# Order of the first tiles in a ternary feed-forward kernel: q between x's first tiles, x's third half transposed and summed, c's first halves rounded on GpSimd

## The reference

```python
q_emb = relu(cond @ W3 + b3)                      # 128 x 256
v_sum = sum(x, axis=1)                            # over the 32 places of a sequence
c = relu(((32 * x + v_sum) * q_emb[:, None]) @ W2 + b2)

def ternary_quant(w):                             # value used: -s, 0 or s
    s = mean(abs(w)); return clip(round(w / s), -1, 1) * s
h1 = c @ ternary_quant(w1).T
h3 = c @ ternary_quant(w3).T
out = x + (silu(h1) * h3) @ ternary_quant(w2).T
```

## Time and profile before

| | us |
|---|---|
| median of 3 runs | 166.16 |
| profiled execution, its own time | 166.31 |
| span of its profile | 164.5 |
| TensorE busy | 160.6 (98%) |
| VectorE busy | 116.1 (71%) |
| ScalarE busy | 88.9 (54%) |
| GpSimd busy | 55.2 (34%) |

### The profile page before, as it was taken

The page is one execution under the profiler, slowest core; times in us unless marked ns, Lnnn a source line. Parts: engine busy times, 40 slices in busy tenths (PEclk is TensorE's granted clock), DMA queues, the critical chain, the costliest instruction groups (busy, mean ns, idle before and its releaser), DMA issues.

```text
span 164.5 us, 2291 instructions
## 1 busy us (share of the span) xinstructions
PE 160.6 (98%) x765; PEld 132.5 (81%) x765; DVE 116.1 (71%) x186; ACT 88.9 (54%) x163; POOL 55.2 (34%) x52
## 2 busy tenths in 40 slices
PE   7999999999999999999999999999999999999992
PEld 3988777888887888788887888788887888788892
DVE  2166999988978891888548891888647880666863
ACT  3148788525744566355744566255744567255540
POOL 5014033321361266204841266203841267001600
PEclk9999999999999999999999999999999999999999
DMA  5998656666566597000160006000160006100063
GB/s 155 298 357 158 103 81 96 97 98 100 90 98 96 91 234 130 11 4 0 23 104 0 0 4 112 17 0 0 22 108 4 2 0 108 19 0 4 15 112 128
DMA packets 67412, 12.67 MB, mean 77 GB/s; under 512 B 63216, under 2 KB 67144, under 8 KB 67400
## 3 DMA queue, kind: packets, MB, share of 16 engines
q1 hardware_dynamic: 67104, 12.33, 38.1%
q10 hardware_dynamic: 296, 0.20, 0.5%
HBM read 8.32 MB, written 4.19 MB: 76 GB/s over the span
## 4 chain that ended last, share of the span: by engine, by line
PE 98%; DVE 0%; issue 0%
PE bank L516 49%; PE bank L559 21%; PE bank L444 17%; PE bank L543 3%; PE bank L429 3%; PE bank L478 1%; PE bank L459 1%; PE bank L491 1%; PE bank L471 0%; PE bank L453 0%; DVE xo L746 0%; PE bank L481 0%; PE bank L483 0%; PE bank L487 0%; DVE blank L688 0%
## 5 line engine op out<-in xcount | busy, mean ns | idle before, releaser
L516 PE MATMUL bank<-c_hi,T 128*128 128x512 f32 (+1 forms) x176 | 69.2, 393 | 0.0
L516 PE MATMUL bank<-c_lo,T 128*128 128x512 f32 (+1 forms) x176 | 68.8, 391 | 0.0
L380 ACT ACTIVATE silu<-bank,checked 128x512 f32<-128x512 f32 (+1 forms) x48 | 33.1, 689 | 51.5 <-PE bank L516 51.3
L731 DVE SCALAR_TENSOR_TENSOR gf<-bank,out_scale,silu 128x512 f32<-128x512 f32 (+1 forms) x42 | 31.3, 744 | 34.4 <-PE bank L516 30.8
L516 PEld LDWEIGHTS bank<-c_hi,T 128*128 128x128 f32 (+1 forms) x176 | 32.7, 186 | 7.6 <-issue 0.2
L516 PEld LDWEIGHTS bank<-c_lo,T 128*128 128x128 f32 (+1 forms) x176 | 32.8, 186 | 7.3
L268 POOL TENSOR_TENSOR x<-y,qT 128x512 f32<-128x512 f32 x12 | 13.7, 1144 | 53.3 <-DVE y L649 53.3
L444 PE MATMUL bank<-x,W_sb 128*128 128x256 f32 x128 | 29.3, 380 | 0.0
L559 PE MATMUL bank<-g_hi,T 128*128 128x512 f32 x70 | 28.5, 407 | 0.0
L739 DVE TENSOR_TENSOR g_lo<-gf,g_hi 128x512 fp32r<-128x512 f32 x40 | 28.4, 711 | 0.0
L387 ACT CAST g_hi<-gf 128x512 fp32r<-128x512 f32 x40 | 24.5, 612 | 5.4 <-DVE gf L731 5.1
(11 more groups left out here) (71 smaller groups left out, 113.9 us busy)
## 6 DMA issues: line engine op xcount, KB each, us to landing
xb<-in_x_dram SPq DMA_DIRECT2D x64, 64.0 KB, 2.5
out_dram<-turned SPq DMA_DIRECT2D x28, 128.0 KB, 2.7
xo<-in_x_dram SPq DMA_DIRECT2D x3, 256.0 KB, 4.3
w_sb<-in_L_ffn_w_dram SPq DMA_DIRECT2D x2, 384.0 KB, 5.9
w_sb<-in_L_ffn_w_dram SPq DMA_DIRECT2D x1, 682.0 KB, 7.7
w_sb<-in_L_ffn_w_dram SPq DMA_DIRECT2D x2, 256.0 KB
xo<-in_x_dram SPq DMA_DIRECT2D x1, 512.0 KB, 3.9
xo<-in_x_dram SPq DMA_DIRECT2D x2, 128.0 KB, 2.6
```

The costliest lines, as they stand in the source:

```text
L380: nc.scalar.activation(silu[r, m % 2, :], h1[j % 2][r], ACT.Silu, scale=checked[r, 0:1]).then_inc(silu_done, 1)
L516: last = pe.matmul(dst[j % 2][0:w, :], T13[:, k, col:col + w], part[:, g % NC, k, :], start=(i == 0), stop=(i == len(passes) - 1))
L731: nc.vector.scalar_tensor_tensor(out=gf[r, m % 3, :], in0=second, scalar=out_scale[r], in1=silu[r, m % 2, :], op0=ALU.mult, op1=ALU.mult). ...
```

## The change

- TensorE: the two matmuls of q and the transpose of the biases come between the two tiles of `mix_x(0)`, q first. Two blank matmuls follow `mix_x(0)`. `mix_x(2)` moves behind `project_c(0)`.
- The third half (`SUMMED = 2`) is no longer multiplied by `mix`: TensorE only transposes its four blocks (with the identity), and VectorE sums them over the sequence, adds 32 x, and multiplies by q from SBUF.
- `c_hi` of the first two halves is written by GpSimd, ahead of each `c_lo`, and no longer by VectorE.
- The first half of `w1`'s absolute sum goes from VectorE to ScalarE, behind `relu(0)`.
- SyncE issues the load of `W2` ahead of the load of x's third half, and does its two semaphore increments for `o_free` after these loads, not ahead of all.

```diff
@@ sync
-            for free in o_free:
-                sp.sem_inc(free, 1)
...
             load_half(1)
+            sp.dma_start(W2_sb[:], W2.rearrange("(c p) n -> p c n", p=P)).then_inc(got_W2, 16)
             load_half(2)
-            sp.dma_start(W2_sb[:], W2.rearrange("(c p) n -> p c n", p=P)).then_inc(got_W2, 16)
+            for free in o_free:
+                sp.sem_inc(free, 1)
@@ gpsimd
             for n in range(EARLY):
-                pool.wait_ge(early_hi_done, n + 1)
+                if n < HALVES:
+                    pool.wait_ge(relu_done, DC * (n + 1))
+                    nc.gpsimd.tensor_copy(half_of(c_hi, n), ct[:, n % NCT]).then_inc(first_hi_done, 1)
+                    pool.wait_ge(first_hi_done, n + 1)
+                else:
+                    pool.wait_ge(early_hi_done, n - HALVES + 1)
@@ scalar
             relu(0)
+            abs_sum(0, w1_sb, 0, got_w1[0], 16)
             abs_sum(0, w1_sb, 1, got_w1[1], 32)
@@ tensor, mix_x(n)
                 for t in range(HTT):
+                    if n == 0 and t == 1:
+                        project_q()
+                        transpose_b()
...
+                        if n == SUMMED:
+                            last = pe.transpose(there, rows, ident[:])
+                        else:
+                            last = pe.matmul(there, rows, mix[:], start=True, stop=True)
@@ tensor
             mix_x(0)
-            pe.wait_ge(got_b, 16 * 2)
-            pe.transpose(b_cols_ps, b_rows[:], ident[0:2 * DC, 0:2 * DC]).then_inc(b_cols_done, 1)
...
+            keep_busy(2)
             mix_x(1)
-            mix_x(2)
             pe.wait_ge(got_W2, 16)
             project_c(0)
+            mix_x(2)
             project_c(1)
@@ vector, scale_mixed(n)
+                if n == SUMMED:
+                    dve.wait_ge(y_done, 1)
+                whole = flat(y[:, n % 2]) if n == SUMMED else mixed_of(n)
+                nc.vector.tensor_tensor(by_batch(flat(x1[:, n % 2])), by_batch(whole),
                                         over_sequence(flat(qT[:, n])), ALU.mult).then_inc(x1_done, 1)
@@ vector
             scale_mixed(0)
             scale_mixed(1)
-            abs_sum(0, w1_sb, LOADED * D, got_w1[0])
-            scale_mixed(2)
-            early_hi(0)
+            sum_sequence(SUMMED)
+            add_sum(SUMMED)
+            scale_mixed(SUMMED)
             limit(0)
             above_limit(0, w1_sb, w1_t, parts[0])
             scale_mixed(3)
-            early_hi(1)
```

More of the change, by code:

```diff
@@ L41, in adaln_ternary_ffn_kernel @@
     EARLY = AHEAD * HALVES
+    SUMMED = 2
     NCT = 4
@@ L167, in adaln_ternary_ffn_kernel @@
         checked_done = sem("checked_done")
-        early_hi_done, early_lo_done = sem("early_hi_done"), sem("early_lo_done")
+        first_hi_done, early_hi_done, early_lo_done = sem("first_hi_done"), sem("early_hi_done"), sem("early_lo_done")
         wT_done = sem("wT_done")
@@ L264, in scale_by_q @@
             def scale_by_q(n):
-                pool.wait_ge(y_done, n - EARLY + 1)
+                pool.wait_ge(y_done, n - EARLY + 2)
                 pool.wait_ge(z_done, n - 1)
@@ L427, in mix_x, with project_q, transpose_b @@
                     for c in range(DC):
[L428 to L431, removed]
-                last.then_inc(mixed_done, 1)
+                        there = mixed[:, c * HT + t * P:c * HT + (t + 1) * P]
+                        rows = kept(n // HALVES)[:, n % HALVES * HTT + t, c * P:(c + 1) * P]
+                        if n == SUMMED:
+                            last = pe.transpose(there, rows, ident[:])
+                        else:
+                            last = pe.matmul(there, rows, mix[:], start=True, stop=True)
+                last.then_inc(mixed_done, 1)
+            def project_q():
+                pe.wait_ge(got_W3, 16)
+                pe.wait_ge(condT_copied, 1)
+                for c in range(DC):
+                    pe.matmul(qT_ps[:, c, :], W3_sb[:, c * P:(c + 1) * P], condT[:], start=True, stop=True
+                              ).then_inc(q_done, 1)
+            def transpose_b():
+                pe.wait_ge(got_b, 16 * 2)
+                pe.transpose(b_cols_ps, b_rows[:], ident[0:2 * DC, 0:2 * DC]).then_inc(b_cols_done, 1)
             def project_c(n):
@@ L448, in sum_partitions @@
             def sum_partitions(k):
-                if k != 1:
-                    pe.wait_ge(first_abs_done, 1 + k // 2)
-                pe.wait_ge(abs_done, (1, 3, 4)[k])
+                if k == 2:
+                    pe.wait_ge(first_abs_done, 1)
+                pe.wait_ge(abs_done, (2, 4, 5)[k])
                 pe.matmul(sums_ps[k], ones[:], abs_sums[:, k, :], start=True, stop=True).then_inc(sums_done, 1)
@@ L481, in _, with keep_busy @@
             pe.transpose(condT_ps, cond_sb[:], ident[:]).then_inc(condT_done, 1)
-            for _ in range(2):
-                pe.matmul(bank[:, 7, 0:P], blank[:], blank[:], start=True, stop=True)
+            def keep_busy(n):
+                for _ in range(n):
+                    pe.matmul(bank[:, 7, 0:P], blank[:], blank[:], start=True, stop=True)
+            keep_busy(2)
             pe.wait_ge(mix_ready, 6)
             mix_x(0)
-            pe.wait_ge(got_b, 16 * 2)
-            pe.transpose(b_cols_ps, b_rows[:], ident[0:2 * DC, 0:2 * DC]).then_inc(b_cols_done, 1)
[L488 to L492, removed]
+            keep_busy(2)
             mix_x(1)
-            mix_x(2)
             pe.wait_ge(got_W2, 16)
             project_c(0)
+            mix_x(2)
             project_c(1)
@@ L626, in scale_mixed @@
             def scale_mixed(n):
-                dve.wait_ge(mixed_done, n + 1)
+                if n != SUMMED:
+                    dve.wait_ge(mixed_done, n + 1)
                 if n >= 2:
                     dve.wait_ge(z_done, n - 1)
-                nc.vector.tensor_tensor(by_batch(flat(x1[:, n % 2])), by_batch(mixed_of(n)),
+                if n == SUMMED:
+                    dve.wait_ge(y_done, 1)
+                whole = flat(y[:, n % 2]) if n == SUMMED else mixed_of(n)
+                nc.vector.tensor_tensor(by_batch(flat(x1[:, n % 2])), by_batch(whole),
                                         over_sequence(flat(qT[:, n])), ALU.mult).then_inc(x1_done, 1)
@@ L635, in transpose_x, with transposed, nth_summed @@
                 if n >= EARLY + 2:
-                    dve.wait_ge(y_done, n - EARLY - 1)
+                    dve.wait_ge(y_done, nth_summed(n - 2))
                 nc.vector.transpose(flat(xT[:, n % 2]), flat(xb[:, n])).then_inc(xT_done, 1)
+            def transposed(n):
+                return mixed_of(n) if n == SUMMED else flat(xT[:, n % 2])
+            def nth_summed(n):
+                return 1 if n == SUMMED else n - EARLY + 2
             def sum_sequence(n):
-                dve.wait_ge(xT_done, n - EARLY + 1)
-                nc.vector.tensor_reduce(vsum[:, n % 2, :], by_batch(flat(xT[:, n % 2])), AX.X, ALU.add).then_inc(vsum_done, 1)
+                if n == SUMMED:
+                    dve.wait_ge(mixed_done, n + 1)
+                else:
+                    dve.wait_ge(xT_done, n - EARLY + 1)
+                nc.vector.tensor_reduce(vsum[:, n % 2, :], by_batch(transposed(n)), AX.X, ALU.add).then_inc(vsum_done, 1)
             def add_sum(n):
-                dve.wait_ge(vsum_done, n - EARLY + 1)
-                if n >= 2 + EARLY:
-                    dve.wait_ge(x1_done, n - 1)
+                dve.wait_ge(vsum_done, nth_summed(n))
+                if n >= EARLY:
+                    dve.wait_ge(x1_done, max(n - 1, SUMMED + 1))
                 nc.vector.scalar_tensor_tensor(
-                    out=by_batch(flat(y[:, n % 2])), in0=by_batch(flat(xT[:, n % 2])), scalar=float(S),
+                    out=by_batch(flat(y[:, n % 2])), in0=by_batch(transposed(n)), scalar=float(S),
                     in1=over_sequence(vsum[:, n % 2, :]), op0=ALU.mult, op1=ALU.add).then_inc(y_done, 1)
```

## The result

The changed kernel takes 166.75 us (median of 22 runs, 166.05 to 168.35), the kernel before 166.15 (22 runs, 165.56 to 168.29): a ratio of 1.0051, 95% interval 1.0032 to 1.0071. It is slower by 0.5%, just clear of zero and just beyond the 0.3% that I had called no change.

What follows compares the result with a forecast made beforehand. TensorE was taken to bound the kernel, full up to `h1`. Reordering and cheaper transposes gave -0.10 us, the third product's wait for GpSimd +0.42, sum +0.32: forecast 166.5 us, range 165.9 to 167.0.

Steps and rivals of the forecast that it cites:

- The mechanism that I gave the highest chance: Ahead of the third projection: one lost wait of VectorE's third-half product for GpSimd, 0.24 to 0.72 us; chance 0.57.
- The wait for GpSimd: VectorE's third-half product with q waits out GpSimd's first subtraction, ends 0.55 us behind it; TensorE loses 0.42 us.
- my formula: Price of the third product's wait as a function of GpSimd's cast time C: C - 0.28 us.
- The transposes at half of the cost: Third half, behind the first projection: four transpose records take 0.46 us instead of 0.93 with `mix`, plus 0.10 for switching.
- That GpSimd doesn't keep VectorE out twice: Against the rival that `above_limit` of `w1` also waits out GpSimd's next cast and subtraction: 167.3 us, chance 0.08.
- The semaphore increments of SyncE: SyncE's first loads: moving the increments behind them makes loads 0.1 us earlier, which nothing waits for; effect 0.
- The same 8 + 1 + 4 records: TensorE from 3.53 to 6.69: `mix_x(0)`, biases and q reordered at the same cost; 0, range 0 to +0.2 us.
- `W2` at no gain: Even issued as before, `W2` lands at 7.66, ahead of the first projection's start at 7.82.
- that TensorE is full up to `h1`: TensorE's timeline to `h1` at 17.33 has no hole above about 0.15 us, so VectorE's wait for q costs nothing.
- what would upset it: Sign of being wrong: records halve their time at a different moment, moving all that follows by half that difference.

Runs made afterwards that it cites:

- the version with both edits: Changed kernel with SyncE's increments ahead of its loads again and GpSimd's first subtraction held until VectorE's third-half product with q: 165.76 us, ratio 0.9967.

## Why the prediction was right, and where it wasn't

The time of 166.75 lies in the range, and the sign is that of the forecast; 166.5 is also the median of the changed kernel's usual executions. The mechanism that I gave the highest chance is shown: its row, its hole, and the 0.47 us that come back when GpSimd is held. But the sum came out by two misses of opposite sign, +0.3 and -0.3, and that they nearly cancel was luck.

- *The wait for GpSimd*: right. The cast took 0.61 (I took 0.70 between 0.52 and 1.27), the product 1.47, ending 0.57 behind the subtraction (0.55). VectorE was ready 0.35 us behind the start of the subtraction in the usual profile (I had 0.3). The hole is 0.34 (0.42, or by my formula at 0.61, 0.33). Removing the collision gave 0.47 in the times and 0.41 in the traces, from the first projection to `h1`; that this is my 0.42 again is in part chance, since I had the cast 0.09 too long.
- *The transposes at half of the cost*: right. Four records in 0.43 us at the fast level, and exchanging them for `mix` against the wait changed the time by no more than the scatter (0.1).
- *That GpSimd doesn't keep VectorE out twice*: right. They alternate.
- *"The semaphore increments of SyncE: 0.1 us earlier loads, for nothing that is waited for. All these at 0"*: wrong, by 0.3 us. The load of x's first tile, issued 0.13 us sooner, pushed cond's landing from 2.2 to 2.6 us. TensorE had next to nothing to spare there: before, cond landed at about 2.93 and its transpose followed the blanks at 3.09; after, it landed at about 3.33 and the transpose began at 3.49. That cost 0.3 us in the usual executions of this order (0.30 without the held subtraction, 0.25 with it). I had looked at who waits for the earlier loads, and not at which other loads land near them. What the two loads share, so that one holds up the other, no run here shows.
- *"The same 8 + 1 + 4 records ... in another order, at the same cost", and `W2` at no gain*: wrong. With the two faults taken out the change is 0.4 us faster than the kernel before, where I had 0.1. q between the tiles is worth 0.7 in that version, `W2` ahead about 0.45. These two don't add up: the kernel before has neither and is only 0.4 slower, not 1.15, so each is the price of going without it while the other is there. The step that failed is the first: that TensorE is full up to `h1`. It is full in the one execution that I had, in which its records halve their time at 6.7. By the lengths of the rows in the 13 other profiles this comes between 3.7 and 5.5 us in seven, between 6.7 and 7.1 in four, and near 10 in the two late ones. Where it comes early TensorE is through with its work sooner than the loads, q's relu and the first product, and waits for them: 0.56 us for the product in one, 0.33 for the biases in another. What shortens that chain then pays. I had also asked only `W3` whether it comes in time for q between the tiles (it was waited for in one profile of nine, 0.61 us), and not the biases: they were waited for in five of those nine, 0.26 to 0.45 us.
- *The late executions*: not forecast, only named as what would upset it. In the changed kernel's late profile the slow level lasts into the first projection, at 9.13. That is some 3 us longer than in the earlier trace rows, which at half speed is 1.5 us and more; the heaps are 1.7 apart. They came in 12 of 58 executions of the three versions in which the changed order, the late increments and five blanks meet (the changed kernel and the experiments that hold the subtraction or bring back `mix`). In the six versions of the changed kernel with the increments first (one has TensorE's order of before) they came in 2 of 72, and with six blanks in 0 of 12. So what makes them frequent in the changed order is most likely the delay of cond's transpose by 0.4 us, with TensorE idle in front of it; that is argued from these counts and not shown by a trace. It isn't needed for a late execution: the kernel before has 8 of 120 without it, and the late profile of the version with both edits shows none. That filling the stretch helps as ending it does rests on 12 executions, where a fifth would have made two or three, and is less sure. The Trainium skill (TensorE: Matmul & The Clock Gate, Part 1) says that the gate opens at a moment that differs from run to run of one kernel; the profiles here agree: from about 4.6 to some 10 us in the two of the changed kernel, and from 3.7 us on over all versions. Why the same increments made no late ones in the order before stays open; 12 runs may simply have missed them.

The median of all runs was 0.6 us above the kernel before. By the above, 0.3 to 0.4 of it is the shift of the usual executions, and the rest the share of late ones.

## What to carry to other kernels

One profile is one execution: where the speed of an engine changes at a moment that differs from run to run, "the engine is full" is a statement on that run, and a chain that is hidden in one bounds the next. A cheap instruction ahead of a load sets when that load starts, and here this moved the landing of another queue's load, so a step that moves issues is priced by all loads that land near them. And before an operation is given to GpSimd, look at which VectorE operation with two inputs in SBUF stands beside it; one wait that puts the less urgent of the two behind was worth 0.5 us here.

## What the runs showed of the hardware that I had not expected

A GpSimd cast of 128x512 from float32 took 0.61 us, half of its subtraction (1.27) and near a fill (0.52). A load of 64 KB issued at 0.73 took 0.4 us longer when another queue's first load was issued 0.13 us sooner, at 0.74 instead of 0.87. In the changed order an idle stretch on TensorE of less than half a microsecond near 3 us went with late executions in 12 of 58, against 2 of 72 without it; in the order before it went with 0 of 12.
